# Attention B with the projections of tiles 2 to 5 placed one step earlier, their turned q and k in other banks, and two small scalings on another engine

## What is computed

```
w = (qw.astype(float32) - 8.0) * repeat(scales, 128, axis=0)
q, k, v = x @ w_q, x @ w_k, x @ w_v          # 32, 8 and 8 heads of 128
q, k = rope(q), rope(k)                      # x * cos + rotate_half(x) * sin
attn = softmax(where(causal, q @ k.T / sqrt(128), min))
out = (attn @ v) @ w_o
```

## Time and profile before

| | us |
|---|---|
| median of 3 runs | 1569.1 (1567.02 to 1569.83) |
| the profiled execution | 1571.05 |
| its span, first to last instruction | 1569.2 |
| PE busy | 1469.0 (94%) |
| DVE busy | 1237.7 (79%) |
| ACT busy | 868.9 (55%) |
| POOL busy | 237.6 (15%) |

### The profile page before, as it was taken

The page is one execution under the profiler, slowest core; times in us unless marked ns, Lnnn a source line. Parts: engine busy times, 40 slices in busy tenths (PEclk is TensorE's granted clock), DMA queues, the critical chain, the costliest instruction groups (busy, mean ns, idle before and its releaser), DMA issues.

```text
span 1569.2 us, 23528 instructions
## 1 busy us (share of the span) xinstructions
PE 1469.0 (94%) x7932; PEld 698.8 (45%) x7932; DVE 1237.7 (79%) x2583; ACT 868.9 (55%) x1468; POOL 237.6 (15%) x174
## 2 busy tenths in 40 slices
PE   5779999999999997899999999998999999999988
PEld 3412333333333354455555555554555555555534
DVE  4288888888886388787897887887887888878873
ACT  2205767676778324565665665664665665646630
POOL 2002000000000132221212212212212212211020
PEclk9957999999999998999999999999999999999989
DMA  3894000000000233566576575675684674653621
GB/s 97 150 143 134 1 1 0 0 0 0 0 0 11 64 94 98 105 140 144 121 137 139 120 150 127 129 147 120 128 160 111 141 145 110 134 96 67 115 54 54
DMA packets 352234, 144.64 MB, mean 92 GB/s; under 512 B 314680, under 2 KB 324408, under 8 KB 352128
## 3 DMA queue, kind: packets, MB, share of 16 engines
q1 hardware_dynamic: 352144, 143.48, 43.8%
HBM read 59.64 MB, written 6.19 MB: 42 GB/s over the span
## 4 chain that ended last, share of the span: by engine, by line
PE 73%; DVE 14%; ACT 6%; DMA 3%; issue 3%; SPq 0%; POOL 0%; DVEq 0%; ACTq 0%
PE ps L1433 9%; PE ps L1215 9%; PE ps L1435 9%; PE ps L1434 9%; PE ps L1268 7%; PE ps L1254 7%; PE ps L1395 4%; PE ps L1514 3%; PE ps L1516 3%; PE ps L1515 3%; ACT hl L680 2%; DVE hl L1038 2%; PE ps L1358 2%; DMA scratch<-pieces 2%; PE ps L1458 2%
## 5 line engine op out<-in xcount | busy, mean ns | idle before, releaser
L672 ACT ACTIVATE x<-ps,nmb,factor 128x128 f32<-128x128 f32 (+7 forms) x256 | 211.6, 832 | 290.9 <-DVE nmb L1023 290.9
L823 DVE TENSOR_REDUCE mx<-ps 128x1 f32<-128x512 f32 x512 | 326.4, 686 | 52.8 <-PE ps L1215 49.4
L581 ACT ACTIVATE proj<-ps 128x1024 f32<-128x1024 f32 x256 | 248.4, 1021 | 105.7 <-PE ps L1254 104.8
L1215 PE MATMUL ps<-ks,qs 96*128 (+1 forms) x512 | 200.1, 414 | 16.3 <-DVE mx L823 8.5
L1038 DVE SCALAR_TENSOR_TENSOR hl<-x,rden,hl 128x128 f16<-128x128 f32 (+7 forms) x256 | 208.3, 814 | 4.6 <-ACT hl L680 4.3
L680 ACT ACTIVATE hl<-x,rden 128x128 f16<-128x128 f32 (+7 forms) x256 | 184.1, 767 | 23.2 <-DVE rden L1034 22.5
L1021 DVE TENSOR_REDUCE nmr<-ps 128x1 f32<-128x128 f32 (+7 forms) x256 | 191.9, 750 | 0.0
L500 POOL TENSOR_TENSOR tmp<-tmp 128x640 f32<-128x640 f32 x64 | 98.4, 1538 | 532.1 <-DVE tmp L1017 532.1
L1433 PE MATMUL ps<-wh,xTh 128*128 128x256 f16 (+1 forms) x512 | 167.6, 327 | 0.0
L1434 PE MATMUL ps<-wl,xTh 128*128 128x256 f16 (+1 forms) x512 | 167.5, 327 | 0.0
L1435 PE MATMUL ps<-wh,xTl 128*128 128x256 f16 (+1 forms) x512 | 167.4, 327 | 0.0
(11 more groups left out here) (155 smaller groups left out, 2149.6 us busy)
## 6 DMA issues: line engine op xcount, KB each, us to landing
scale<-sp_n SPq DMA_DIRECT2D x32, 384.0 KB, 4.3
st<-in_L_attn_b_qw_q_dram SPq DMA_DIRECT2D x32, 256.0 KB, 2.8
st<-in_L_attn_b_qw_o_dram SPq DMA_DIRECT2D x32, 256.0 KB, 3.0
scale<-so_n SPq DMA_DIRECT2D x32, 256.0 KB, 3.6
qs<-scratch SPq DMA_DIRECT2D x24, 256.0 KB, 8.4
hlT<-hl SPq DMA_TRANSPOSE x256, 3.5
scratch<-pieces SPq DMA_DIRECT2D x5, 768.0 KB, 13.4
xnat<-attn_a_hidden_state_dram SPq DMA_DIRECT2D x8, 256.0 KB, 4.8
```

The costliest lines, as they stand in the source:

```text
L581: nc.scalar.activation(pbuf[:, e % 4, :].rearrange("p (b n) -> p b n", b=2), ps[:, b:b + 2, :], ACT.Exp, scale=float(HD) ** -0.5).then_inc ...
L672: nc.scalar.activation(pr[:, h, 0:n], flat(2 * (h % 2), n), ACT.Exp, bias=nmb[:, h:h + 1], scale=factor[:, par, 0:1], accum_out=den[:, h:h ...
L823: nc.vector.tensor_reduce(mx[:, f, k // 2, k % 2:k % 2 + 1], ps[:, bank(k), :], AX.X, ALU.max).then_inc(s_mx, 1)
L1215: mm(ps[:, bank, :], qs[0:STACK, ds(g * R + h, 1), f * HALF + qt * P:f * HALF + (qt + 1) * P], ks[0:STACK, ds(g, 1), kh * HALF:(kh + 1) * ...
```

## The change

The projection of tile t+2 now stands at the end of step t, for t = 0 to 3, and no longer in step t+1. Tile 1, and tiles 6, 7 and 0, are projected where they were. Turned q and k of tiles 1 to 4 go to banks 1 and 3, so that banks 6 and 7 are free for the projection that follows; those of the other tiles go to banks 6 and 7 as before. In steps t = 0 to 4 VectorE takes the second maximum ahead of the rotation and dequantises behind the turned q and k. In all steps the scaling of the maximum, and the scaling of the sums ahead of the reciprocal, move from VectorE to ScalarE, and `high_part` stands behind the last exponentials instead of ahead of the turned q and k.

```diff
+        def turned_banks(t):
+
+            return (1, 3) if 1 <= t <= T // 2 else (6, 7)
...
+                    act.wait_ge(s_mxb, u * R + h + 1)
+                    nc.scalar.activation(nmb[:, h:h + 1], nmr[:, h:h + 1], ACT.Copy,
+                                         scale=factor[:, par, 0:1]).then_inc(s_nb, 1)
                     act.wait_ge(s_nb, u * R + h + 1)
...
+                def sums(a):
+                    act.wait_ge(s_eb, u * R + 2 * a + 2)
+                    nc.scalar.activation(sums_scaled[:, 2 * a:2 * a + 2], den[:, 2 * a:2 * a + 2], ACT.Copy,
+                                         scale=1.0 / PSCALE).then_inc(s_dn, 1)
...
                 exponentials(0)
                 exponentials(1)
+                sums(0)
...
-                if not last:
-                    high_part(g + 1, t, 1 - par)
                 if not end:
                     turned(u + 1, t2, par if t < T - 1 else 1 - par)
                 exponentials(2)
                 exponentials(3)
+                sums(1)
+                if not last:
+                    high_part(g + 1, t, 1 - par)
...
-                dve.wait_ge(s_mxb, u * R + h + 1)
-                nc.vector.tensor_scalar(nmb[:, h:h + 1], nmr[:, h:h + 1], factor[:, par, 0:1], None,
-                                        ALU.mult).then_inc(s_nb, 1)
...
-                dve.wait_ge(s_eb, u * R + 2 * a + 2)
-                nc.vector.tensor_scalar(rden[:, 2 * a:2 * a + 2], den[:, 2 * a:2 * a + 2], 1.0 / PSCALE, None,
-                                        ALU.mult).then_inc(s_dn, 1)
                 dve.wait_ge(s_dn, u * 2 + a + 1)
-                nc.vector.reciprocal(rden[:, 2 * a:2 * a + 2], rden[:, 2 * a:2 * a + 2]).then_inc(s_rd, 1)
+                nc.vector.reciprocal(rden[:, 2 * a:2 * a + 2], sums_scaled[:, 2 * a:2 * a + 2]).then_inc(s_rd, 1)
...
-                if not last:
+                sooner = t <= T // 2
+                if sooner:
+                    maximum(u, 1, n)
+                elif not last:
                     dequantise(g + 1, t)
...
-                maximum(u, 1, n, par)
+                if not sooner:
+                    maximum(u, 1, n)
...
+                if sooner and not last:
+                    dequantise(g + 1, t)
                 low(u, 1, n)
...
+                    q, k = turned_banks(t)
+                    dst = ps[:, q, h * P:(h + 1) * P] if h < R else ps[:, k, 0:P]
...
-                if not end:
+                if not end and (t == 0 or t > T // 2):
                     project_all(u + 1, *after(g, t), par if t < T - 1 else 1 - par)
...
+                if t < T // 2:
+                    project_all(u + 2, g, t + 2, par)
```

More of the change, by code:

```diff
@@ L165, in build @@
             rden = scoped(mem, "rden", [P, R])
-            scoped(mem, "gap", [P, P])
+            sums_scaled = scoped(mem, "sums_scaled", [P, R])
+            scoped(mem, "gap", [P, P - R])
             wh, wl = (scoped(mem, f"w{c}", [P, 2, KC, BW], F16) for c in "hl")
@@ L644, in turned @@
                 act.wait_ge(s_qkT, v + 1)
-                nc.scalar.activation(qTh[:, t % 2].rearrange("p h n -> p (h n)"), ps[:, 6, :], ACT.Copy,
+                nc.scalar.activation(qTh[:, t % 2].rearrange("p h n -> p (h n)"), ps[:, turned_banks(t)[0], :], ACT.Copy,
                                      scale=HEADROOM / (XSCALE * WSCALE)).then_inc(s_qke, 1)
                 c = k_slot(t, par) * P
-                nc.scalar.activation(kTh[:, c:c + P], ps[:, 7, 0:P], ACT.Copy,
+                nc.scalar.activation(kTh[:, c:c + P], ps[:, turned_banks(t)[1], 0:P], ACT.Copy,
                                      scale=HEADROOM / (XSCALE * WSCALE)).then_inc(s_qke, 1)
@@ L1017, in rope_sin, with maximum @@
                 nc.vector.tensor_tensor(o[:, :, HALF_D:], rotary_in()[:, :, 0:HALF_D], sn, ALU.mult).then_inc(s_rope, 1)
-            def maximum(u, h, n, par):
+            def maximum(u, h, n):
                 dve.wait_ge(s_sc, u * R + h + 1)
                 nc.vector.tensor_reduce(nmr[:, h:h + 1], flat(2 * (h % 2), n), AX.X, ALU.max, negate=True).then_inc(s_mxb, 1)
-                dve.wait_ge(s_mxb, u * R + h + 1)
-                nc.vector.tensor_scalar(nmb[:, h:h + 1], nmr[:, h:h + 1], factor[:, par, 0:1], None,
-                                        ALU.mult).then_inc(s_nb, 1)
             def group_factor(g, par):
@@ L1043, in turned @@
                 dve.wait_ge(s_qke, v * 2 + 2)
-                nc.vector.scalar_tensor_tensor(qTl[:, t % 2].rearrange("p h n -> p (h n)"), ps[:, 6, :],
+                nc.vector.scalar_tensor_tensor(qTl[:, t % 2].rearrange("p h n -> p (h n)"), ps[:, turned_banks(t)[0], :],
                                                HEADROOM / (XSCALE * WSCALE), qTh[:, t % 2].rearrange("p h n -> p (h n)"),
@@ L1047, in turned @@
                 c = slice(k_slot(t, par) * P, (k_slot(t, par) + 1) * P)
-                nc.vector.scalar_tensor_tensor(kTl[:, c], ps[:, 7, 0:P], HEADROOM / (XSCALE * WSCALE), kTh[:, c],
+                nc.vector.scalar_tensor_tensor(kTl[:, c], ps[:, turned_banks(t)[1], 0:P], HEADROOM / (XSCALE * WSCALE), kTh[:, c],
                                                ALU.mult, ALU.subtract).then_inc(s_ql, 1)
@@ L1077, in step @@
                     dve.wait_ge(s_fcr, g + 1)
-                maximum(u, 0, n, par)
+                maximum(u, 0, n)
                 if exists(*one):
                     low(u - 1, 3, (one[1] + 1) * P)
-                if not last:
+                sooner = t <= T // 2
+                if sooner:
+                    maximum(u, 1, n)
+                elif not last:
                     dequantise(g + 1, t)
@@ L1089, in step @@
                     values_low(u + 1, par if t < T - 1 else 1 - par, t2)
-                maximum(u, 2, n, par)
+                maximum(u, 2, n)
                 low(u, 0, n)
-                maximum(u, 3, n, par)
+                maximum(u, 3, n)
                 if not end:
@@ L1451, in project_all, with turn_b @@
                 project(v, t, 0, par).then_inc(s_pj, 1)
-            def turn_b(v):
+            def turn_b(v, t):
                 pe.wait_ge(s_rpa, v + 1)
@@ L1536, in step @@
                 if not end:
-                    turn_b(u + 1)
+                    turn_b(u + 1, after(g, t)[1])
                 if exists(*one):
                     values(*one, par if t >= 1 else 1 - par)
+                if t < T // 2:
+                    project_all(u + 2, g, t + 2, par)
             project_all(0, 0, 0, 0)
             tokens(2, 4, 5)
-            turn_b(0)
+            turn_b(0, 0)
             tokens(2, 6, 7)
```

1 line of the change is left out of this document (removed).

## The result

The changed kernel takes 1575.32 us (median of 13 executions, 1569.45 to 1580.57), the kernel before on the same chip 1569.11 (13 executions, 1566.47 to 1577.58). The ratio is 1.004, with a 95% interval of 1.0024 to 1.0056: 6.2 us slower, where I had forecast 8 us faster, and outside my range. The profiled execution took 1576.22 us with a span of 1574.4; in it the mean granted clock was 0.970, against 0.972 before. Over the 13 executions the time moves against the clock: 0.963 in the longest (1580.57), 0.972 in the shortest, and 0.963 to 0.973 in all.

The account below looks back on a forecast made before the run. TensorE was taken as the bound. Groups 1 to 6 gain 0.95 us each (5.7), group 0 gains 3, last group loses 0.1, tail 0.3: 8.3 us, profiled 1571.05 to 1562.8, median 1561; range 1550 to 1570.

Parts of the forecast that it names:

- Moving the projection: Keys of tile 1 to keys of tile 5: 43.3 us plus 3.9 moved ahead, 47.2 against 48.38, 1.2 us less a group.
- kT waits: Keys of tiles 2 to 4 waiting for turned k's low part, 1.58 to 0.34 us late; claimed to go.
- the chain: Steps 1 to 4, keys through maxima, rotation and GpSimd to the turning: 4.85 us at t = 1, 0.55 more each tile.
- one of the things that I had said would show me wrong: Keys of heads 2 or 3 waiting for exponentials in steps 1 to 7.
- Step 0 ... I take 0: Step 0: head 3's 1.02 us wait goes, but `values` of tile 7 still awaits the last transposing transfer; gain 0.
- my cases: Four: own forecast 0.58, 1553 to 1567; waits vanish 0.12, 1540; new waits take all 0.17, 1570; ScalarE late 0.13, 1582.
- at most 0.3 a group: Step 0: upper bound in us on the gain, which was itself taken as 0.
- the late steps: Step 4 onward: ScalarE's 1.4 us more ahead of the context's high part delays later work; 0.25 us wait at t = 5.
- The scalings' size: Small scaling on ScalarE: 0.28 us, plus 0.04 for the wait on itself.
- Steps 6 and 7 ... I take 0: Steps 6 and 7: lag less than step 5 after the late `high_part`; loss 0, at most 0.3 us each.
- Group 0: First group of attention B: tile 2's projection fills a hole where TensorE idles at half clock; 3 us gained.
- 638.8: Group 0: predicted time in us of step 2's keys, against 638.33 before, with tile 3's projection already done.

Follow-up runs that it names:

- e7: The changed kernel with twelve throw-away matmuls added ahead of `values` in step 0, the real projection staying in place; 1565.78 us, ratio 0.9986.
- e4: The changed kernel with both small scalings back on VectorE in all steps; 1582.40 us, ratio 1.0080.
- e5: e2 with both small scalings back on VectorE in steps 5 to 7 only; 1550.19 us, ratio 0.9891.
- e6: e2 with `high_part` back ahead of the turned q and k in steps 5 to 7; 1555.01 us, ratio 0.9918.
- e2: The changed kernel with half of tile 2's projection (q, 12 matmuls) moved ahead of `values` in step 0; 1554.31 us, ratio 0.9901.
- e3: The kernel before, with only step 0's second maximum moved ahead of rotation and chunk on VectorE; 1581.55 us, ratio 1.0073.
- e1: The changed kernel with step 0 alone back in VectorE's old order (chunk, rotation, second maximum); 1574.92 us, ratio 1.0024.
- e8: The changed kernel with the second maximum behind the rotation again in steps 1 to 4, step 0 untouched; 1580.97 us, ratio 1.0070.

## Why the prediction was wrong

**Moving the projection: right.** From keys of tile 1 to keys of tile 5 I had 43.3 us; 9.94 + 11.46 + 12.36 + 9.69 = 43.45. The kT waits are gone. The turning waits for `tmp` of GpSimd in steps 1 to 4, by the brackets 0.48, 0.32, 0.16 and less, where I had 0.73, 0.64, 0.55 and 0.46. That is how it is counted: the brackets count idle time, mine were distances between starts. By starts the chain is right: the turning begins 4.80, 5.66, 5.92 and 6.50 us after the keys, where it gave 4.85, 5.40, 5.95 and 6.50. The miss at t = 2 is the 0.24 us that head 2's keys wait there for an exponential, one of the things that I had said would show me wrong.

**"Step 0 ... I take 0": this is the step that failed.** That the start of `values` would not come sooner was right. What I left out is that the wait ahead of it has a second price, the clock behind it. Step 0 of group 3 took 21.34 us where I had 19.40. Of these 1.94 us, 1.50 are the clock. It is 1.44 to 1.68 us in each of six groups, 9.6 us together, and e7 gives back 9.5. The other 0.44 are a later landing, below. Without the fall of the clock the kernel stands at e7's 1565.8, inside my range and 2.5 us under the kernel before of its comparison. So the sign was decided by a mechanism that was in none of my cases. My "at most 0.3 a group" bounded only a shift of the landing.

**The landing: 0.44 us later in group 3, 0.06 to 0.53 and 0.29 in the mean of seven groups, which I hadn't.** ScalarE has the scaling of the sums and the high part of `woh` ahead of the context's high part now, as I wrote for the late steps, but I did not follow it into step 0. The context's high part starts 0.48 us after the keys of tile 0, before 0.26:

```profile
943.05 0.20 ACT L685 ACTIVATE sums_scaled<-den 128x2 f32<-128x2 f32 x1
943.16 0.61 ACT L607 ACTIVATE woh<-st 128x512 f16<-128x512 f32 x1
943.68 0.58 ACT L661 ACTIVATE cTh<-ps 128x512 f16<-128x512 f32 x1
```

Behind it hang `low` of head 2 and the last two transfers, issued at 946.6 and 948.6, 3.4 and 5.4 us after the keys, where the earlier trace rows gave 3.24 and 5.2; the last one also takes 5.2 us to land instead of 4.9:

```profile
L464 SPq DMA_TRANSPOSE hlT<-hl x2: 1879/2259/2639, 946.6 to 948.6; - x2
...
DMA to landing us min/median/max: 4.4/4.8/5.2
```

In e4, without the scalings on ScalarE but with the late high part, `values` starts 10.30 to 10.40 us after the keys again in five of seven groups, and 0.07 us later than before in the mean of seven. So most of the delay comes from the scalings. Landings vary by some 0.3 us from group to group in every kernel (10.25 to 10.59 before, 10.52 to 10.84 after).

**The scalings' size: right; "Steps 6 and 7 ... I take 0": wrong in size.** One takes 0.29 us (I had 0.28), that of the sums 0.20, and the exponential behind one starts 0.04 us after its end, as I had for the wait on itself:

```profile
L677 ACT ACTIVATE nmb<-nmr,factor 128x1 f32<-128x1 f32 x256 | 74.4, 291 | 165.7 <-DVE nmr L1036 165.0
...
L685 ACT ACTIVATE sums_scaled<-den 128x2 f32<-128x2 f32 x128 | 26.0, 203 | 4.0
```

The first agrees with the estimate of 0.28 from the Trainium skill ("ScalarE: Activation LUTs", What ACT_TABLE_LOAD costs). Its rule for `mul`, VectorE and not ScalarE, holds here for steps 6 and 7 alone; for the whole kernel e4 measured the contrary, 7 us. Step 5 came as forecast (14.62 for 14.65). Steps 6 and 7 cost 0.32 and 0.21 more, about my upper bound of 0.3 each; I had put this on the high part, and e5 and e6 show that it is the scalings.

**Group 0: the number met by luck.** The keys of group 1 come at 719.62 instead of 722.80, 3.2 us sooner for a forecast of 3. But attention B's first keys already come at 612.62 instead of 613.88, in a stretch that the change doesn't touch. So 1.26 of the 3.2 us are not the change's, and group 0 itself gained 1.9. The miss is there by the keys of tile 2: they come 26.0 us after the first keys, where my 638.8 meant 24.9.

**The sum of the profiled executions**, against 1571.05: ahead of attention B -1.3 (forecast 0); group 0 -1.9 (-3); groups 1 to 6 together +7.8 (-5.7), a miss of 13.5: the clock in five of them 7.9, the landing 1.7 (0.28 in the mean of the six), steps 6 and 7 6 x 0.53 = 3.2, steps 1 to 4 6 x 0.15 = 0.9; group 7 up to the keys of its last tile +2.0 (+0.1); the last step and what follows -1.4 (+0.3). That is +5.2, the measured difference.

Of the -1.4, some 0.4 comes with a shorter wait of the last output projection for `cTl`, 1.48 us instead of 1.98. The rest is the clock once more, the other way round. In the kernel before it falls behind that single wait of 1.98 us, and from the first to the twelfth matmul's start it takes 3.65 us; in the changed kernel, behind 1.48 us, the clock holds and it takes 2.38. The next waits hide 0.3 of these 1.27 us, and from 1514 us on the two traces run alike. The rows are of the kernel before:

```profile
1497.95 0.39 PE L1433 MATMUL ps<-woh,cTh 128*128 128x512 f16 x1 [1.98 <-DVE cTl L1062]
...
1499.04 0.63 PE L1435 MATMUL ps<-woh,cTl 128*128 128x512 f16 x1
```

**What stays open.** That the loss is the clock in step 0 behind TensorE's waits, and that work put into the wait keeps it, is shown by e2, e3 and e7. Which waits suffice is not. Here is the idle time of TensorE from 4 us after the keys of tile 0 up to `values`, summed from the brackets of the timeline, for groups 1 to 6:

| kernel | idle, us | clock fell in |
|---|---|---|
| e7 | 0.95 to 1.20 | none |
| before | 1.71 to 2.14 | none |
| e3 | 2.09 to 2.36 | all six |
| e1 | 2.07 to 2.52 | all but group 1 |
| e4 | 1.98 to 2.31 | groups 1, 3, 5 |
| after | 2.20 to 2.53 | all but group 1 |
| e8 | 2.24 to 2.54 | group 1 alone |

Only e7 stands apart. (These are steps 0 alone; at the end of attention B the kernel before does lose its clock, behind one wait of 1.98 us.) The other ranges overlap: the kernel before keeps its clock behind 2.14 us, in e4 it falls behind 2.00 us and holds behind 2.31, and e8 has the waits of the changed kernel. That is not the chance of one execution: the six executions of e8 have mean clocks of 0.972 to 0.976, the thirteen of the changed kernel 0.963 to 0.973. The two kernels differ in the order of VectorE in steps 1 to 4 alone, and from step 5 up to `values` TensorE's instructions are the same. Something besides the length of these waits decides, and no run tells what. Code that no edit touches varies too: from 90 to 155 us, ahead of attention B, the granted clock is 0.66 in the trace of the kernel before, 0.68 in the changed kernel's and 0.72 in e2's and e7's, and e7 reaches attention B 5.0 us sooner than the kernel before (1.2 of them by a shorter wait for a transfer). Falls that come and go would account for executions of the changed kernel that lie 11 us apart, since step 0 with or without the fall differs by 1.5 us, seven times, and the stretch ahead of attention B by up to 5. The kernel before has such executions too (1582.37 us at a mean clock of 0.965, where most have 0.975). Only one execution of each kernel was traced, so this is argued and not shown.

## What to carry to other kernels

A wait of the bounding engine may be priced at more than its length: here a matmul stretch behind waits of 2.0 to 2.5 us ran 1.4 to 1.7 us longer, so a change that leaves a wait "as long as it was" can still cost. When work is moved off a place that waits, look whether it, or anything at hand, can be put into the longest wait left; moving half a projection there turned 0.4% slower into 1.0% faster, and 1.1% with the small scalings put on the engine that has time at each step, though the intervals of these two overlap. A single trace can also meet a forecast by chance: compare stretches from their own first instruction, since here up to 5 us of difference lay ahead of the changed code. Follow every instruction that is put in front of a chain into all the steps that it runs in, not only into the one in which it looked late.

## What the runs showed of the hardware

TensorE's granted clock fell from 2.4 to 1.2 GHz behind idle time of 2.0 to 2.5 us in one to three pieces with work between them (e1: 1.05, 0.42 and 0.68 us), the longest 2.1 us (e3). It cost 1.4 to 1.7 us each time on the 24 matmuls that followed. With waits equal to 0.1 us it falls in one kernel and holds in another, or falls in one group and holds in the next. Adding twelve useless matmuls a group to the changed kernel took its ratio from 1.0040 to 0.9986. In code that no edit touched, the mean granted clock of one stretch (90 to 155 us) lay between 0.66 and 0.72 from kernel to kernel. A scaling of a single column costs 0.29 us on ScalarE where that of two columns by a constant costs 0.20.
